# Layer 1's attention logits: rows added by TensorE, the bend split between ScalarE and VectorE

## The chip, the cores and the metric

The kernel runs on one core of one Trainium2 chip. The metric is the device time of one execution in microseconds, and the median of several executions is compared. The trace is of one execution of its own.

## The reference, cut to what matters

A network of four layers (a graph part and a feed-forward part in each) runs over 3125 nodes with 256 features and 50,000 edges sorted by destination. The change touches one part alone, the edges of layer 1's graph attention (4 heads of 64 features):

```
xl = x @ W_l + b_l          # per node, gathered by the edge's source
xr = x @ W_r + b_r          # per node, taken at the edge's destination
e  = xl[src] + xr[dst] + edge_attr_16 @ W_e
e  = leaky_relu(e, 0.2)     # "the bend"
logit = sum(e * att, over the 64 features of a head)
# then softmax of the logits over the edges of one destination,
# and the sum of xl[src] times those shares, per destination
```

## The kernel before, in words

The edges lie in slots, in pairs of 2 x 128 edges that belong to one block of 128 destinations. A batch is two pairs, that is 512 edges or four tiles of 128 (`BATCH` 4, `TWO` 2), and there are 110 batches. The function `gat_edges` does layer 1 (tiles named `l1e_`) and layer 3 (`l3e_`). It is written by hand as one instruction order for each engine. `skewed` takes a list of steps with lags and unrolls five batches in one loop round: in the round for batch t, a step of lag 2 works on batch t - 2. Semaphores tie the engines together, and each engine runs its own list strictly in order. A batch goes through these steps:

- SyncE loads the records (`l1e_rec`) and the edge attributes, turned and split in bf16 parts (`l1e_attrT`). GpSimd writes the indices of the sources, marks the first two tiles of the one-hot matrix of destinations (L1088), and issues four indirect DMAs that gather the rows of xl (`l1e_rows`, L1054). VectorE marks the other two tiles (L1096, "the one-hot half").
- TensorE turns the one-hot tiles (`l1e_ps_hot`). ScalarE copies them twice from PSUM (`l1e_outside` L3332 and `l1e_nodehot` L3333, "the one-hots' copies").
- TensorE sums xr[dst] (L3449) and the attribute part (L3450) into `l1e_ps_x`, 256 columns for each of four tiles ("the sums").
- VectorE adds the gathered rows (`join`, L3459), one instruction of 512 columns for each pair, and bends in place (`bend`, L3464), again one for each pair.
- GpSimd multiplies by the attention vector (L3481), and VectorE reduces to logits (L3486).
- TensorE turns the logits into rows, four units for each batch ("the logits' rows", L3291 and L3294, two head pairs for each of two pairs of tiles). VectorE takes the largest of each unit (L3208, "the tops"), raises the running top (L3216, L3223) and forms the factors by which old sums shrink (L3225, L3228, "the shrinks").
- TensorE spreads the tops back to the edges (L3311, "the spread"). VectorE subtracts them from the logits (L3233, L3236, "the fall"). ScalarE exponentiates (L3341) and weighs the gathered rows with 16 copies of 64 columns and 4 small ones (L3350, L3352, "the weighing").
- TensorE sums the weighted rows by destination (L3305, "the weighted sums"), VectorE adds them to the running totals (L3249), and ScalarE flushes these (L3366, L3367).

VectorE's order within one round is: one-hot half, tops of the first two units, raise, join of pair 0, tops of the last two units, raise and shrinks, join of pair 1, both bends, totals, fall, totals, logits. TensorE's is: rows of the logits of pair 1, weighted sums, spread, sums, rows of the logits of pair 0, turned one-hots. In any round the joins belong to the batch after the one whose tops are taken, and the sums on TensorE to the batch after that.

Of the kernel before, what the change touches and what calls it, by code (L numbers as in the profile page):

```python
# [12 lines left out]
ALU = mybir.AluOpType  # L13
ACT = mybir.ActivationFunctionType
# [998 lines left out]
class Gather:  # L1013
# [5 lines left out]
    def __init__(self, s, net, placed, table, width, lo):  # L1019
# [8 lines left out]
        self.half_ready = s.sem("half_ready")  # L1028
# [44 lines left out]
    def find(self, eng, q, i, b):  # L1073

        eng.wait_ge(self.rec_loaded[b], i * 16 + 16)
        eng.tensor_copy(self.idx[b][:, :], self.column(b, self.placed.far)).then_inc(self.idx_ready, 1)  # L1076
# [4 lines left out]

    def hot_tiles(self, eng, q, i, b, tick):
        eng.wait_ge(self.rec_loaded[b], i * 16 + 16)
        eng.wait_ge(self.hot_free, q + 1)
        eng.sem_inc(tick, 1)
        eng.tensor_copy(self.idx[b][:, :], self.column(b, self.placed.far)).then_inc(self.idx_ready, 1)
        for k in range(BATCH // 2):
            ins = eng.tensor_scalar(at(self.onehot[b], k, P), self.net.columns[:, :], self.column(b, self.placed.near, k),  # L1088
                                    None, ALU.is_equal)
        ins.then_inc(self.hot_ready, 1)  # L1090

    def hot_half(self, eng, q, i, b):
        wide = [P, BATCH // 2, P]
        eng.wait_ge(self.rec_loaded[b], i * 16 + 16)
        eng.wait_ge(self.hot_free, q + 1)
        eng.tensor_tensor(tiled(self.onehot[b][:, :], P)[:, BATCH // 2:BATCH, :],  # L1096
                          self.net.columns[:, :].unsqueeze(1).to_broadcast(wide),
                          self.column(b, self.placed.near)[:, BATCH // 2:BATCH].unsqueeze(2).to_broadcast(wide), ALU.is_equal)\
            .then_inc(self.half_ready, 1)
# [2015 lines left out]
def gat_edges(net, name, heads, each, table, lo, logits_of, tops=None):  # L3115
# [11 lines left out]
    with ExitStack() as ctx:  # L3127
# [136 lines left out]
        def _(pe):  # L3264
# [5 lines left out]
            def turn(q, i, b):  # L3270
                pe.wait_ge(g.hot_ready, q + 1)
                if UNITS > 1:
                    pe.wait_ge(g.half_ready, q + 1)
# [48 lines left out]
        def _(act):  # L3322
# [46 lines left out]
            skewed(act, (3, shrinks), (3, weigh), (0, turn), (4, flush))  # L3369


class L1Logits:
# [5 lines left out]
    by_pair = True  # L3378

    def __init__(self, net, xr, att, s, g, ps_x, nodehot, logit, logit_ready, nodehot_ready):  # L3380
# [6 lines left out]
        self.e = [s.sb(f"e{k}", [P, 2 * D]) for k in range(TWO)]  # L3387
        self.loaded = s.sem("we_loaded")
# [19 lines left out]
    def gather(self, pool):  # L3408
        skewed(pool, (0, lambda q, i, b: self.g.hot_tiles(pool, q, i, b, self.pool_tick)), (0, lambda q, i, b: self.g.gather_batch(pool, q, b)),
               (2, lambda q, i, b: self.multiply(pool, q)))  # L3410
# [4 lines left out]
    def hot(self, dve, q, i, b):  # L3415
        self.g.hot_half(dve, q, i, b)
# [22 lines left out]
    def tensor(self, pe, q, i, b):  # L3439
# [837 lines left out]
```

## Time and profile before

| what | us |
|---|---|
| median of 3 runs | 6451.83 (6433.74 to 6451.86) |
| the profiled execution | 6440.41 |
| its span | 6439.0 |
| edges of layer 1: first sums to last logits | 2326.8 to 3401.8 |

| engine, whole span | busy |
|---|---|
| TensorE matmul | 76% |
| VectorE | 67% |
| TensorE weight load | 58% |
| GpSimd | 48% |
| ScalarE | 43% |

Shares over the whole span mix eight stages. The change lies in the stage of layer 1's edges alone, about a sixth of the time, so what counts is read there: how long a batch takes, which engine waits for which, and what is late last. The records of TensorE's matmuls last longer than the spacing of two of them, since they overlap in the pipe. The price of one more matmul is therefore taken from the spacing of starts and not from the mean record.

### The profile page before, as it was taken

The page shows a single profiled execution, that of the slowest core. Times are in us where ns is not written, and L with a number is a line of the kernel's source. Part 1 is how long each engine was busy: PE and PEld are TensorE (multiplying, and loading weights), DVE is VectorE, ACT ScalarE, POOL GpSimd, SP SyncE. Part 2 cuts the span into 40 slices and gives each one's busy share as a digit, 9 for nine tenths or more (in the row PEclk, how much of TensorE's full clock was granted, in tenths as well). Part 3 has the DMA queues.
Part 4 walks back from the last instruction along what each step waited for, and adds up shares of the span by engine and source line. Part 5 has one row for each costly group of instructions (what it writes and reads, how often), then busy time and mean ns, then how long its engine had stood idle before and what let it go on. Part 6 is the DMA issues. An engine that isn't in the chain of part 4 may idle for free. (4 is left out here: it accounts for less than half of the span.)

```text
span 6439.0 us, 120316 instructions
## 1 busy us (share of the span) xinstructions
PE 4915.4 (76%) x25586; PEld 3702.7 (58%) x25587; DVE 4325.7 (67%) x13269; ACT 2736.8 (43%) x8015; POOL 3093.6 (48%) x3493
## 2 busy tenths in 40 slices
PE   5621999994574578888883899969989997888595
PEld 4510777763453356666663566645657775666484
DVE  7770888873786679999997777753433335888613
ACT  0010877773114336666662111124523333887421
POOL 4786777776474048888880222213210001777221
PEclk9975999997696689999995899989989998999697
DMA  6522444455586222222231555543520002666453
GB/s 237 179 65 58 122 120 121 120 113 102 137 252 150 62 57 70 66 70 68 68 66 48 167 186 187 183 129 113 147 79 10 10 10 66 161 159 159 75 172 108
DMA packets 843340, 719.85 MB, mean 112 GB/s; under 512 B 405662, under 2 KB 749251, under 8 KB 842660
## 3 DMA queue, kind: packets, MB, share of 16 engines
q1 hardware_dynamic: 596280, 372.06, 20.5%
q0 software_dynamic: 120064, 280.26, 16.7%
q10 hardware_dynamic: 126828, 65.67, 3.5%
q8 instruction: 59, 0.97, 0.1%
q14 instruction: 109, 0.89, 0.0%
HBM read 521.19 MB, written 201.60 MB: 112 GB/s over the span
## 5 line engine op out<-in xcount | busy, mean ns | idle before, releaser
L1054 POOL DMA_INDIRECT l3e_rows<-table,l3e_idx x440 | 436.0, 991 | 736.6 <-DVE l3e_idx L1076 608.9
L1054 POOL DMA_INDIRECT l0e_rows<-table,l0e_idx x440 | 448.8, 1020 | 150.0 <-issue 132.0
L1054 POOL DMA_INDIRECT l1e_rows<-table,l1e_idx x440 | 430.6, 979 | 121.4 <-issue 121.4
L3350 ACT ACTIVATE l1e_weighted<-l1e_rows,l1e_power 128x64 f32<-128x64 f32 x1760 | 462.9, 334 | 16.7 <-ACT l1e_power L3341 9.3
L824 POOL DMA_INDIRECT records_by_src<-l0n_rec_src,l0n_pos_at_src x390 | 399.4, 1024 | 115.3 <-issue 109.1
L1331 PE MATMUL l0e_ps_w<-l0e_wf,l0e_hidT 128*128 128x256 f32 x1760 | 417.3, 391 | 34.8 <-DVE l0e_shifted L1272 34.7
L1331 PEld LDWEIGHTS l0e_ps_w<-l0e_wf,l0e_hidT 128*128 128x128 f32 x1760 | 331.3, 193 | 162.5 <-issue 87.0
L3291 PE MATMUL l1e_ps_row<-net_ident,l1e_logit 128*128 128x128 f32 x1760 | 276.8, 280 | 128.9 <-DVE l1e_logit L3486 127.5
L2673 ACT ACTIVATE l1fg_hT<-l1fg_ps_h,l1fg_b_cols 128x256 f32<-128x256 f32 x256 | 107.5, 471 | 530.0 <-PE l1fg_ps_h L2616 529.9
L2055 ACT ACTIVATE l2fe_hT<-l2fe_ps_h,l2fe_own,l2fe_own 128x320 f32<-128x320 f32 x320 | 197.6, 618 | 309.7 <-PE l2fe_ps_h L2005 309.4
L3305 PE MATMUL l3e_ps_s<-l3e_weighted,l3e_onehot 128*128 128x257 f32 x880 | 250.4, 430 | 92.2 <-ACT l3e_weighted L3352 92.2
L3481 POOL TENSOR_TENSOR l1e_e<-l1e_e,l1x_att 128x512 f32<-128x512 f32 x220 | 274.8, 1271 | 84.9 <-DVE l1e_e L3464 84.8
L3291 PEld LDWEIGHTS l1e_ps_row<-net_ident,l1e_logit 128*128 128x128 f32 x1760 | 192.5, 137 | 209.7 <-issue 154.7
L2108 DVE SCALAR_TENSOR_TENSOR net_x<-l2fe_ps_y,l2fe_mix,net_x 128x256 f32 x200 | 96.8, 484 | 309.0 <-PE l2fe_ps_y L2017 309.0
L3851 PE MATMUL l2d_ps<-l2d_wide,net_work 128*128 128x512 f32 (+2 forms) x800 | 290.1, 518 | 8.3 <-DVE l2d_wide L3902 5.9
L2788 POOL DMA_INDIRECT outputs<-l1fg_y,l1fg_target x64 | 70.5, 1102 | 467.5 <-DVE l1fg_y L2725 455.9
L3208 DVE TENSOR_REDUCE l1e_tile_top<-l1e_ps_row 128x2 f32<-128x512 f32 x440 | 287.3, 685 | 4.2 <-PE l1e_ps_row L3294 2.7
L2616 PE MATMUL l1fg_ps_h<-l1fg_xT,l1fg_w_in 128*128 128x256 f32 x1024 | 264.8, 381 | 1.7 <-DVE l1fg_xT L2713 0.8
L3449 PE MATMUL l1e_ps_x<-l1x_xr,l1e_nodehot 128*128 x880 | 255.7, 393 | 2.7 <-ACT l1e_nodehot L3333 2.7
L3305 PEld LDWEIGHTS l3e_ps_s<-l3e_weighted,l3e_onehot 128*128 128x128 f32 x880 | 162.9, 204 | 159.4 <-ACT l3e_weighted L3352 141.9
L3769 POOL DMA_DIRECT2D l2d_counts<-counts x192 | 108.2, 564 | 279.2 <-ACT l2d_wide L3961 139.8
L2630 PE MATMUL l1fg_ps_y<-l1fg_w_out,l1fg_hT 128*128 128x256 f32 x1024 | 231.2, 379 | 0.0
(830 smaller groups left out, 14840.9 us busy)
## 6 DMA issues: line engine op xcount, KB each, us to landing
counts<-l1f_total ACTq DMA_DIRECT2D x272, 128.0 KB, 4.0
l1fg_w_in<-in_L_ffn_W SPq DMA_DIRECT2D x32, 1024.0 KB
l1fg_w_out<-in_L_ffn_W SPq DMA_DIRECT2D x32, 1024.0 KB
records_by_dst<-l0n_blank_dst SPq DMA_DIRECT2D x5, 6512.0 KB
l3e_rec<-records_by_dst SPq DMA_DIRECT2D x110, 296.0 KB, 3.1
l2d_counts<-counts SPq DMA_DIRECT2D x208, 128.0 KB, 2.7
l2d_counts<-counts POOLq DMA_DIRECT2D x192, 128.0 KB, 2.8
l3fg_w_in<-in_L_ffn_w SPq DMA_DIRECT2D x16, 1024.0 KB, 7.5
```

The source lines that it names most:

```text
L824: pool.indirect_dma_start(self.to.records, bass.IndirectOffsetOnAxis(self.pos_at[b][:, j:j + 1], 0), at(self.rec[b], j, self.to.width), No ...
L1054: pool.indirect_dma_start(at(self.rows[b], k, self.width), None, self.table, bass.IndirectOffsetOnAxis(self.idx[b][:, k:k + 1], 0)).then_i ...
L1331: ins = pe.matmul(ps_w[:, k, m * D:(m + 1) * D], hidT[b][:, c * WIDE + (2 * k + m) * P:c * WIDE + (2 * k + m + 1) * P], at(wf2, c, D), sta ...
L2616: ins = pe.matmul(ps_h[:, n % HALVES, (m % 2) * SLICE:(m % 2 + 1) * SLICE], w_in[b][:, c * F + m * P:c * F + (m + 1) * P], at(xT[b], c, SL ...
L2630: ins = pe.matmul(ps_y[:, t, 0:D], hT[b][:, c * SLICE + t * P:c * SLICE + (t + 1) * P], at(w_out[b], c, D), start=c == 0, stop=c == FC - 1)
L3208: dve.tensor_reduce(tile_top[:, c:c + w], tiled(ps_row[:, side, 0:w * PAIR], PAIR), AX.X, ALU.max)\
L3291: pe.matmul(ps_row[:, side, lo:lo + P], logit[b][:, c:c + 1].to_broadcast([P, P]), net.ident[:, :], is_transpose=True, start=h == h0 and m ...
L3305: ins = pe.matmul(ps_s[:, k, 0:W], at(g.onehot[b], m, P), at(weighted, m, W), start=m == 2 * k, stop=m > 2 * k)
L3350: act.activation(out[:, h, 0:each], g.rows[b][:, lo:lo + each], ACT.Copy, scale=power[b][:, m * heads + h:m * heads + h + 1])
L3449: pe.matmul(out, at(self.nodehot[b], 2 * k + m, P), at(self.xr, self.block[k], D), start=True, stop=False)
L3481: pool.tensor_tensor(e, e, self.att[:, :].unsqueeze(1).to_broadcast([P, 2, D]), ALU.mult).then_inc(self.times_att, 1)
L3851: ins = pe.matmul(ps[0:k_in, n % 2, 0:width(g)], lhsT, wide[k % WIDE][:, 0:width(g)], start=t == 0, stop=False)
```

## The change

Four things change, all in layer 1's edges:

1. TensorE adds the gathered rows. After the two products for a tile comes a third, the identity times the tile's rows (f32, 256 columns), into the same PSUM sum. There are four more products for each batch, and TensorE waits for the gathered rows first.
2. ScalarE takes the positive part: for each pair one Relu with scale 0.8 from `l1e_ps_x` into a new tile `l1e_above`. This step stands between the weighing and the one-hots' copies.
3. VectorE has one join for each pair: 0.2 times the PSUM sum plus `l1e_above`. Adding the rows and the two bends are gone. GpSimd's multiply waits for this join.
4. The one-hot is marked whole by VectorE (128x512 in one instruction, L1009) and no longer half by GpSimd.

```diff
 class Gather:
-    def hot_tiles(self, eng, q, i, b, tick):      # indices, two tiles of the one-hot
-    def hot_half(self, eng, q, i, b):             # the other two
+    def find(self, eng, q, i, b, tick=None):      # indices alone
 ...
             def turn(q, i, b):                    # TensorE
                 pe.wait_ge(g.hot_ready, q + 1)
-                if UNITS > 1:
-                    pe.wait_ge(g.half_ready, q + 1)
 ...
-            skewed(act, (3, shrinks), (3, weigh), (0, turn), (4, flush))
+            skewed(act, (3, shrinks), (3, weigh), *([(1, lambda q, i, b: logits.bend(act, q, i, b))] if logits.bends else []),
+                   (0, turn), (4, flush))
 ...
 class L1Logits:
     def gather(self, pool):
-        skewed(pool, (0, lambda q, i, b: self.g.hot_tiles(pool, q, i, b, self.pool_tick)), (0, lambda q, i, b: self.g.gather_batch(pool, q, b)),
+        skewed(pool, (0, lambda q, i, b: self.g.find(pool, q, i, b, self.pool_tick)), (0, lambda q, i, b: self.g.gather_batch(pool, q, b)),
                (2, lambda q, i, b: self.multiply(pool, q)))
     def hot(self, dve, q, i, b):
-        self.g.hot_half(dve, q, i, b)
+        dve.wait_ge(self.g.rec_loaded[b], i * 16 + 16)
+        self.g.hot(dve, q, i, b)
     def tensor(self, pe, q, i, b):
+        self.g.wait_rows(pe, i, b)
         for k in range(TWO):
             n = q * TWO + k
             pe.wait_ge(self.x_read, n + 1)
             for m in range(2):
                 out = self.ps_x[:, k, m * D:(m + 1) * D]
                 pe.matmul(out, at(self.nodehot[b], 2 * k + m, P), at(self.xr, self.block[k], D), start=True, stop=False)
-                ins = pe.matmul(out, at(self.attrT[b], 2 * k + m, P), self.we_parts[:, :], start=False, stop=True)
+                pe.matmul(out, at(self.attrT[b], 2 * k + m, P), self.we_parts[:, :], start=False, stop=False)
+                ins = pe.matmul(out, self.net.ident[:, :], at(self.g.rows[b], 2 * k + m, D), start=False, stop=True)
             ins.then_inc(self.sums, 1)
-    def join(self, dve, q, b, k):
-        dve.wait_ge(self.sums, q * TWO + k + 1)
-        dve.tensor_tensor(self.e[k][:, :], self.ps_x[:, k, 0:2 * D], at(self.g.rows[b], k, 2 * D), ALU.add).then_inc(self.x_read, 1)
-    def bend(self, dve, q, k):
-        e = self.e[k][:, :]
-        dve.wait_ge(self.x_read, q * TWO + TWO + k + 1)
-        dve.scalar_tensor_tensor(e, e, self.SLOPE, e, ALU.mult, ALU.max).then_inc(self.bent, 1)
+    def bend(self, act, q, i, b):
+        for k in range(TWO):
+            act.wait_ge(self.sums, q * TWO + k + 1)
+            act.activation(self.above[k][:, :], self.ps_x[:, k, 0:2 * D], ACT.Relu, scale=1.0 - self.SLOPE).then_inc(self.bent, 1)
+    def join(self, dve, q, k):
+        dve.wait_ge(self.bent, q * TWO + k + 1)
+        dve.scalar_tensor_tensor(self.e[k][:, :], self.ps_x[:, k, 0:2 * D], self.SLOPE, self.above[k][:, :], ALU.mult, ALU.add)\
+            .then_inc(self.x_read, 1)
     def multiply(self, pool, q):
-        pool.wait_ge(self.bent, q * TWO + TWO)
+        pool.wait_ge(self.x_read, q * TWO + 2 * TWO)
```

TensorE, the sums of one pair of tiles, of the kernel before and then of the changed one:

```order
L3449 MATMUL l1e_ps_x<-l1x_xr,l1e_nodehot 128x256
L3450 MATMUL l1e_ps_x<-l1e_we_parts,l1e_attrT 128x256
L3449 MATMUL l1e_ps_x<-l1x_xr,l1e_nodehot 128x256
L3450 MATMUL l1e_ps_x<-l1e_we_parts,l1e_attrT 128x256
L3446 REGISTER_ALU
```

```order
L3434 MATMUL l1e_ps_x<-l1x_xr,l1e_nodehot 128x256
L3435 MATMUL l1e_ps_x<-l1e_we_parts,l1e_attrT 128x256
L3436 MATMUL l1e_ps_x<-l1e_rows,net_ident 128x256
L3434 MATMUL l1e_ps_x<-l1x_xr,l1e_nodehot 128x256
L3435 MATMUL l1e_ps_x<-l1e_we_parts,l1e_attrT 128x256
L3436 MATMUL l1e_ps_x<-l1e_rows,net_ident 128x256
L3431 REGISTER_ALU
```

One product with the identity has come in for each tile, two for each pair and four for each batch. Nothing else of TensorE's order has moved.

ScalarE, the end of the weighing and what follows it, before and then changed (`l1e_above` is the positive part):

```order
L3350 ACTIVATE l1e_weighted<-l1e_rows,l1e_power 128x64 x4
L3352 ACTIVATE l1e_weighted<-l1e_power 128x4
L3331 ISA
L3332 ACTIVATE l1e_outside<-l1e_ps_hot 128x512
L3333 ACTIVATE l1e_nodehot<-l1e_ps_hot 128x512
```

```order
L3330 ACTIVATE l1e_weighted<-l1e_rows,l1e_power 128x64 x4
L3332 ACTIVATE l1e_weighted<-l1e_power 128x4
L3445 ISA
L3446 ACTIVATE l1e_above<-l1e_ps_x 128x512
L3445 REGISTER_ALU
L3446 ACTIVATE l1e_above<-l1e_ps_x 128x512
L3311 ISA
L3312 ACTIVATE l1e_outside<-l1e_ps_hot 128x512
L3313 ACTIVATE l1e_nodehot<-l1e_ps_hot 128x512
```

The two positive parts stand ahead of the copies, and the copies and the flush move back by two instructions.

VectorE, from the shrinks to the first tops of the next round, before and then changed:

```order
L3228 SCALAR_TENSOR_TENSOR l1e_shrink<-l1e_top,l1e_fresh 128x4
L3458 REGISTER_ALU
L3459 TENSOR_TENSOR l1e_e<-l1e_ps_x,l1e_rows 128x512
L3463 REGISTER_ALU
L3464 SCALAR_TENSOR_TENSOR l1e_e<-l1e_e 128x512
L3463 REGISTER_ALU
L3464 SCALAR_TENSOR_TENSOR l1e_e<-l1e_e 128x512
L3249 SCALAR_TENSOR_TENSOR l1e_total<-l1e_total,l1e_shrink,l1e_ps_s 128x65 x4
L3233 TENSOR_TENSOR l1e_ps_top<-l1e_logit,l1e_ps_top 128x16
```

```order
L3210 SCALAR_TENSOR_TENSOR l1e_shrink<-l1e_top,l1e_fresh 128x4
L3450 REGISTER_ALU
L3451 SCALAR_TENSOR_TENSOR l1e_e<-l1e_ps_x,l1e_above 128x512
L3231 SCALAR_TENSOR_TENSOR l1e_total<-l1e_total,l1e_shrink,l1e_ps_s 128x65 x4
L3215 TENSOR_TENSOR l1e_ps_top<-l1e_logit,l1e_ps_top 128x16
```

The two bends are gone from between the second join and the totals. The joins stand where they stood.

## Rows read from the trace of the kernel before

**Rows 1.** Busy time by stretch: PE, PEld, DVE, ACT, POOL (instructions), granted clock, DMA, GB/s.
```profile
2800.00:3000.00 200.00, 173.32 (x1072) 134.46 (x1072) 187.57 (x513) 139.30 (x583) 163.97 (x187) 1.00 0.27 68
```
**Rows 2.** Waits, 2400 to 3370 us: who for whom, total us, times, longest.
```profile
ACT l1e_power L3341 <- DVE l1e_power L3236: 214.6, 100, 2.7
...
PE l1e_ps_row L3291 <- DVE l1e_logit L3486: 107.6, 100, 1.4
...
PE l1e_ps_top L3311 <- DVE l1e_shrink L3228: 20.8, 100, 0.3
```
**Rows 3.** Timeline of VectorE, one batch: start, length, instruction.
```profile
2801.35 0.42 DVE L1096 TENSOR_TENSOR l1e_onehot<-net_columns,l1e_rec 128x256 f32<-128x256 f32 x1
2801.82 1.35 DVE L3208 TENSOR_REDUCE l1e_tile_top<-l1e_ps_row 128x2 f32<-128x512 f32 x2
...
2803.45 0.69 DVE L3459 TENSOR_TENSOR l1e_e<-l1e_ps_x,l1e_rows 128x512 f32<-128x512 f32 x1
2804.06 1.28 DVE L3208 TENSOR_REDUCE l1e_tile_top<-l1e_ps_row 128x2 f32<-128x512 f32 x2
...
2805.75 0.22 DVE L3228 SCALAR_TENSOR_TENSOR l1e_shrink<-l1e_top,l1e_fresh 128x4 f32<-128x4 f32 x1
2805.88 0.68 DVE L3459 TENSOR_TENSOR l1e_e<-l1e_ps_x,l1e_rows 128x512 f32<-128x512 f32 x1
2806.49 1.28 DVE L3464 SCALAR_TENSOR_TENSOR l1e_e<-l1e_e 128x512 f32<-128x512 f32 x2
2807.69 0.85 DVE L3249 SCALAR_TENSOR_TENSOR l1e_total<-l1e_total,l1e_shrink,l1e_ps_s 128x65 f32<-128x65 f32 x4
...
2808.66 0.17 DVE L3236 TENSOR_SCALAR l1e_power<-l1e_ps_top 128x16 f32<-128x16 f32 x1
...
2809.63 0.68 DVE L3486 TENSOR_REDUCE l1e_logit<-l1e_e 128x8 f32<-128x512 f32 x1
```
**Rows 4.** Timeline of TensorE (matmuls), the same batch.
```profile
2800.77 0.65 PE L3291 MATMUL l1e_ps_row<-net_ident,l1e_logit 128*128 128x128 f32 x4 [1.17 <-DVE l1e_logit L3486]
2801.25 0.38 PE L3294 MATMUL l1e_ps_row<-l1e_outside,l1e_ident_bf 128*128 128x512 bf16 x1
...
2803.92 1.92 PE L3305 MATMUL l1e_ps_s<-l1e_weighted,l1e_onehot 128*128 128x260 f32 x8
2806.02 1.05 PE L3311 MATMUL l1e_ps_top<-l1e_top,l1e_nodehot 128*128 128x4 f32 x8 [0.19 <-DVE l1e_shrink L3228]
2806.94 0.68 PE L3449 MATMUL l1e_ps_x<-l1x_xr,l1e_nodehot 128*128 x2
2807.45 0.27 PE L3450 MATMUL l1e_ps_x<-l1e_we_parts,l1e_attrT 128*128 128x256 bf16 x1
2807.56 0.60 PE L3449 MATMUL l1e_ps_x<-l1x_xr,l1e_nodehot 128*128 x2
...
2808.65 0.60 PE L3449 MATMUL l1e_ps_x<-l1x_xr,l1e_nodehot 128*128 x2
...
2810.45 0.65 PE L3291 MATMUL l1e_ps_row<-net_ident,l1e_logit 128*128 128x128 f32 x4 [1.10 <-DVE l1e_logit L3486]
```
**Rows 5.** Timeline of ScalarE: the exponential, and what follows the weighing.
```profile
2808.87 0.22 ACT L3341 ACTIVATE l1e_power<-l1e_power 128x16 f32<-128x16 f32 x1 [2.10 <-DVE l1e_power L3236]
...
2813.70 0.60 ACT L3332 ACTIVATE l1e_outside<-l1e_ps_hot 128x512 bf16<-128x512 f32 x1 [0.20 <-ACT l1e_weighted L3352]
2814.20 0.59 ACT L3333 ACTIVATE l1e_nodehot<-l1e_ps_hot 128x512 f32<-128x512 f32 x1
```
**Rows 6.** Groups by shape, whole span: count, busy us, mean ns, idle before.
```profile
L1009 DVE TENSOR_TENSOR l0e_onehot<-net_columns,l0e_rec 128x512 f32<-128x512 f32 x110 | 75.4, 685 | 0.0
L1263 DVE SCALAR_TENSOR_TENSOR l0e_hidT<-l0e_ps_h,l0e_bf_low,l0e_raised 128x512 f32<-128x512 f32 x220 | 154.4, 743 | 15.8 <-ACT l0e_raised L1371 14.5
L3333 ACT ACTIVATE l1e_nodehot<-l1e_ps_hot 128x512 f32<-128x512 f32 x110 | 65.1, 591 | 0.0
L1365 ACT ACTIVATE l0e_raised<-l0e_ps_h,l0e_bf 128x512 f32<-128x512 f32 x220 | 139.4, 684 | 34.3 <-PE l0e_ps_h L1322 33.7
```

More of the change, by code:

```diff
@@ L1027, in __init__ @@
         self.hot_ready = s.sem("hot_ready")
-        self.half_ready = s.sem("half_ready")
         self.rows_loaded = [s.sem(f"rows_loaded{b}") for b in range(RING)]
@@ L1071, in columns @@
         return self.rec[b][:, k * self.n + c:k * self.n + c + w]
-    def find(self, eng, q, i, b):
+    def find(self, eng, q, i, b, tick=None):
         eng.wait_ge(self.rec_loaded[b], i * 16 + 16)
+        if tick is not None:
+            eng.sem_inc(tick, 1)
         eng.tensor_copy(self.idx[b][:, :], self.column(b, self.placed.far)).then_inc(self.idx_ready, 1)
@@ L1080, in hot @@
         mark_nodes(eng, self.net, self.onehot[b], self.column(b, self.placed.near)).then_inc(self.hot_ready, 1)
-    def hot_tiles(self, eng, q, i, b, tick):
[L1083 to L1090, printed above, removed]
-    def hot_half(self, eng, q, i, b):
[L1093 to L1099, printed above, removed]
     def wait_rows(self, eng, i, b):
@@ L3378 @@
     by_pair = True
+    bends = True
     def __init__(self, net, xr, att, s, g, ps_x, nodehot, logit, logit_ready, nodehot_ready):
@@ L3387, in __init__ @@
         self.e = [s.sb(f"e{k}", [P, 2 * D]) for k in range(TWO)]
+        self.above = [s.sb(f"above{k}", [P, 2 * D]) for k in range(TWO)]
         self.loaded = s.sem("we_loaded")
@@ L3454, in vector_steps @@
         return self.vector_early, self.vector_middle, self.vector_late, self.find, self.hot
-    def join(self, dve, q, b, k):
-        dve.wait_ge(self.sums, q * TWO + k + 1)
-        dve.tensor_tensor(self.e[k][:, :], self.ps_x[:, k, 0:2 * D], at(self.g.rows[b], k, 2 * D), ALU.add).then_inc(self.x_read, 1)
-    def bend(self, dve, q, k):
-        e = self.e[k][:, :]
-        dve.wait_ge(self.x_read, q * TWO + TWO + k + 1)
-        dve.scalar_tensor_tensor(e, e, self.SLOPE, e, ALU.mult, ALU.max).then_inc(self.bent, 1)
+    def bend(self, act, q, i, b):
[6 more added lines that the diff above has]
+            .then_inc(self.x_read, 1)
     def vector_early(self, dve, q, i, b):
-        self.g.wait_rows(dve, i, b)
-        self.join(dve, q, b, 0)
+        self.join(dve, q, 0)
     def vector_middle(self, dve, q, i, b):
-        self.join(dve, q, b, 1)
+        self.join(dve, q, 1)
         dve.sem_inc(self.g.rec_free, 1)
-        self.bend(dve, q, 0)
-        self.bend(dve, q, 1)
     def multiply(self, pool, q):
-        pool.wait_ge(self.bent, q * TWO + TWO)
+        pool.wait_ge(self.x_read, q * TWO + 2 * TWO)
         pool.sem_inc(self.pool_tick, 1)
@@ L4040 @@
     by_pair = False
+    bends = False
     def __init__(self, net, wide, s, g, ps_x, nodehot, logit, logit_ready, nodehot_ready):
```

## The prediction

> **What bounds the kernel now.** I read the table of stretches first. In the stage that the change touches the clock is granted in full (1.00, the 2.4 GHz level), VectorE is busy 187.6 of 200 us, TensorE's matmuls 173.3, GpSimd 164.0 and ScalarE 139.3 [rows 1]. So VectorE looks like the bound, and a change that takes work from it looks right. But 94% busy is not a cycle, so I read the waits next: TensorE waits for the logits 107.6 us in 100 batches, and for the shrinks 20.8 us [rows 2]. Two engines hand the work to and fro, and what counts is the closed chain between them.
>
> The timeline gives that chain. I count from the first row of the logits on TensorE, 2800.77, as 0. The same row comes again at 2810.45 [rows 4], so a batch takes 9.68 us, and 110 batches take 1065 us (the count stands in [rows 6]). Within the batch:
> - 0.86: the first unit's rows are complete (2801.25 + 0.38) [rows 4].
> - 1.05: VectorE's first top starts, as the one-hot half before it ended at 1.00 (2801.77) [rows 3].
> - 1.05 to 5.25: tops, raise, join, tops, raise, shrinks in VectorE's order, until TensorE's spread starts at 2806.02 with a recorded wait of 0.19 for the shrink [rows 3, 4]. That is 4.20 us with no wait of VectorE.
> - 5.25 to 6.17: the spread, until the sums start at 2806.94 [rows 4].
> - 6.17 to 8.42: the sums. The last pair of products starts at 2808.65 and occupies 0.54, so TensorE is free at 2809.19 [rows 4].
> - 8.42 to 9.68: TensorE has nothing, 1.26 us. VectorE is still at the bends (1.28 recorded, 1.20 from start to start), totals, fall and logits [rows 3].
>
> So two things close together: VectorE's own list of 9.7 us, nearly without gaps, and TensorE's list, with 1.26 us of room at its end and 0.2 to 0.3 at the shrinks.
>
> **The change part by part.** All times are for one batch.
>
> *VectorE.* The two bends go: 1.20 (2806.49 to 2807.69) [rows 3]. The join becomes another operation of the same size, one operand in PSUM and one in SBUF. The join now costs 0.61 from start to start and 0.69 recorded [rows 3]. The nearest row of the new kind, in layer 0, costs 743 ns against 685 for a plain one, but it has a scalar in a tile where this one has a number [rows 6]. I take 0.61, with 0.67 as the upper bound. The one-hot grows from 0.42 to the 685 ns of the whole one [rows 3, 6], +0.27. VectorE's list falls from 9.68 to about 8.75, and VectorE no longer sets the pace.
>
> *ScalarE.* Two Relus of 128x512 from PSUM come in. The copy of the same shape takes 591 ns [rows 6] and the exponential with a bias tile 684 [rows 6]. I take 0.60 each, 1.2 in all. ScalarE was busy 139.3 of 200 us, 6.74 for a batch of 9.68 [rows 1], so there is room in total. What they can delay is checked below as a chain. The copies move back 1.2 us: in the walk below they end near 4.0, and the sums that read the turned one-hots begin at 6.0 and want those of a batch that was copied one round earlier. So that costs nothing. The flush behind them then ends near 5.6, before the next exponential at 6.7, which is covered by the 2.1 us that ScalarE waits for the fall now [rows 2, 5].
> The Trainium skill, "ScalarE: Activation LUTs", Rules for kernel authors, sends relu to VectorE and not to ScalarE, with a gain that it states for bf16. The f32 rows here don't bear that out: two bends on VectorE are recorded at 1.28 together [rows 3], and a copy from PSUM on ScalarE at 0.591 [rows 6]. By that page's budget for an ACTIVATE a Relu would be estimated at 0.72 us, which would lengthen the ScalarE chain by 0.12 and still not make it the longest.
>
> *GpSimd.* Its two tiles of the one-hot go, and its multiplies wait for the joins, which come earlier than the bends did. It loses work and gains nothing, so it costs nothing. The gathers keep their place: they are issued a round ahead of the sums that now read the rows, and their issue moves forward. So TensorE's new wait for the rows costs nothing in the steady state. If the rows were late, everything on TensorE would queue behind it (sums, logits' rows, turned one-hots).
>
> *TensorE.* Four f32 products of 256 columns come in. A pair of products (f32 and bf16) takes (2808.65 - 2807.56) / 2 = 0.545, and the bf16 one takes 0.11 of it (2807.45 to 2807.56) [rows 4]. So the f32 one is 0.435, and four are 1.74 us. Lower bound: were they as cheap as the bf16 ones, 4 x 0.11 = 0.44. Upper bound: the first product in the stretch takes 0.51 (2806.94 to 2807.45), so 2.04. I take 1.74, since the weights are f32 as in the row it comes from. No further weight load shows, as loads of the same size already hide behind such products.
>
> **The sum.** The closed chain, with the new prices:
> - first unit's rows complete at 0.86, first top starts at 0.91, since the one-hot is done long before. This saves 0.14 against 1.05.
> - 4.20 to the spread: 5.11.
> - 0.92 for the spread: 6.03.
> - 2.25 + 1.74 = 3.99 for the sums: 10.02.
> - The next logits' rows start at once if the logits are there. The second join starts at 4.97. Then 0.61, totals 0.77, fall 0.40, totals 0.77, first logits 0.68: 8.20. So the logits are 1.8 us early, and the one-hot behind them is done near 9.8, before the next first top at 10.93.
>
> The batch takes 10.02 against 9.68: +0.34, and times 110 it is +37 us. TensorE's wait for the logits vanishes (1.26), but 1.74 comes into the same place, and the saving of 0.14 at the first top covers only part of the difference. VectorE's 0.93 of relief buys nothing more, because VectorE then waits for TensorE.
>
> The ScalarE chain is the other candidate. From the end of the fall (2808.83) to the end of the weighing, where the copies start now (2813.70), it is 4.87 [rows 3, 5]. The first Relu and its hand-over are 0.64. From the join of pair 0 to the end of the fall it is 5.38 now (2803.45 to 2808.83) [rows 3], less 1.20 for the bends, 4.18. The sum is 9.69. This is shorter than 10.02, so the Relu is ready 0.33 before the join wants it.
>
> The start and end of the stage may add or take 2 us. The sum is made against the profiled execution, 6440.4 us, and gives 6477. That execution lies 11 us under the median of the three runs and within their spread. From the median the sum is 6489. I forecast 6482.
>
> **The rivals.**
>
> *A. No change: the wait at the shrinks goes too.* TensorE's own list without any wait is 3.15 from the logits' rows to the weighted sums (2800.77 to 2803.92), 1.77 for these (four products of 260 columns), 0.92 and 3.99: 9.83, less about 0.1 for a wait on a top inside it. With the ScalarE chain at 9.69 the batch would be 9.7 to 9.8, within 10 us of now: 6445 to 6455. For it: only 0.3 us separates the cases, and an f32 product at 0.35 instead of 0.435 would be enough. Against it: VectorE's 4.20 is a string of dependent steps with the join in the middle, and nothing in the change shortens it.
>
> *B. Faster: the busiest engine sets the pace.* VectorE at 94% falls to about 8.75 us a batch. If the added products hide in TensorE's gaps, the batch goes toward that: -0.93 x 110 = -102 us, 6338. It decides the outcome where the chain through TensorE drops under 9.5, which takes products at the lower bound of 0.11 each (chain 8.7), and a weighing that starts earlier as well. The rows speak against it: the same f32 product keeps 0.435 in three pairs in a row, and the ScalarE chain alone holds 9.69.
> The Trainium skill, "Perfetto Trace Analysis", Identifying the Most-Contended Engine, says to optimize the engine of highest occupancy first, and to judge TensorE not by its matmul busy time. By that rule VectorE is the engine to relieve. The waits of this trace [rows 2] put TensorE in the same closed chain.
>
> *C. Slower still: the Relus are late at the join.* A Relu of 0.684 like the exponential [rows 6], joins of 0.67 and a weighing slowed 5% (0.22) by sharing with the neighbours give 9.69 + 0.09 + 0.12 + 0.22 = 10.1, and a wait on it before the join shifts the tops and the spread behind it. With both chains hitting each other, 10.3 is plausible: +0.62 x 110 = +68, 6510 to 6520. For it: the slack is only 0.33 us. Against it: each bound would have to hold at once.
>
> **How the numbers follow.** A measurement of this kernel tells about 0.3%, 19 us, from no change. The forecast case, with 6465 to 6500 as its own range, has a chance of 0.61. Rival C has 0.15, A 0.16 and B 0.08. Slower by over 0.3% is all of C and most of the forecast case, 0.73. Within is A and the low edge of the forecast case, 0.18. Faster is 0.09. The range reaches over A's place and C's: 6444 to 6520. It leaves out B and the ends.
>
> **What would show it.** In the trace of the changed kernel: a batch of 10.0 us; the identity products spaced 0.43; TensorE's wait for the logits gone, its wait for the shrinks still there at 0.2 to 0.4 a batch; VectorE idle 1.2 to 1.5 us a batch before the tops, waiting for TensorE's logit rows, and busy near 81%; no wait of the joins for ScalarE. If the joins wait for the Relu, C is right. If TensorE shows no wait at all and the batch is 9.8, A is right. A batch under 9.5 would overturn the sum.

## The result and the profile after

| | before | after |
|---|---|---|
| median, us | 6447.03 (4 runs, 6433.74 to 6451.86) | 6484.43 (4 runs, 6480.44 to 6492.23) |
| profiled execution, us | 6440.41 | 6480.44 |
| TensorE, VectorE, ScalarE, GpSimd busy | 76, 67, 43, 48% | 79, 65, 44, 45% |
| one batch of layer 1's edges, median | 9.68 | 10.09 |

The ratio is 1.0068, 95% interval 1.0057 to 1.008: slower, by 0.7%. The forecast was 6482, +37 by the sum against the profiled execution; measured are +40.0 there and +37.4 in the medians.

In the traces the stage, from the end of the means' product ahead of it (the last write of `l1n_ps`) to the end of its last weighted sums, goes from 1115.3 us to 1154.2, +38.9. It falls into three parts. From the first spread to the last, 109 batches, it is 1057.1 before and 1098.8 after, +41.7. Behind the last spread nothing changes (8.2). Ahead of the first spread it is 50.0 before and 47.2 after, -2.8: the first sums come 3.8 us later, and the filling of the pipeline from there to the first logits takes 10.8 us instead of 16.6. Outside the stage about 1 us is left, but as the balance of two larger differences: the stages ahead of it are 7.4 us shorter in the second trace, and those behind it 8.3 us longer, though the change touches neither.

The table of stretches of the changed kernel, the same 200 us as [rows 1] and with the same columns:

```profile
2800.00:3000.00 200.00, 196.54 (x1191) 159.22 (x1189) 163.60 (x459) 152.51 (x592) 133.69 (x140) 1.00 0.26 66
```

VectorE fell from 187.6 to 163.6 us, and GpSimd from 164.0 to 133.7. TensorE rose from 173.3 to 196.5, 98% of the stretch. The clock is the same, so the busy times can be compared.

The waits of the changed kernel, from 2400 to 3400 us (who for whom, total, times, longest), to be read against [rows 2]:

```profile
POOL l1e_e L3466 <- DVE l1e_e L3451: 155.3, 99, 1.7
ACT l1e_power L3321 <- DVE l1e_power L3218: 144.2, 99, 1.5
DVE l1e_tile_top L3190 <- PE l1e_ps_row L3274: 132.0, 99, 1.4
...
POOL l1e_rows L1053 <- POOL l1e_idx L1077: 80.4, 99, 0.8
...
PE l1e_ps_top L3291 <- DVE l1e_shrink L3210: 17.2, 99, 0.2
```

The hand-over has turned round. Before, TensorE waited for VectorE's logits, 107.6 us in 100 batches. That wait is gone, and VectorE now waits for TensorE's logits' rows, 1.33 us a batch. The only wait of TensorE's matmuls is the one for the shrinks, 0.17 a batch. GpSimd has a new wait of 0.81 a batch between writing the indices and the first gather, since its one-hot tiles no longer stand between them. Nothing waits for the gathers, so it costs nothing.

VectorE's timeline of one batch, to be read against [rows 3]:

```profile
2800.56 1.34 DVE L3190 TENSOR_REDUCE l1e_tile_top<-l1e_ps_row 128x2 f32<-128x512 f32 x2 [1.24 <-PE l1e_ps_row L3274]
...
2802.19 0.69 DVE L3451 SCALAR_TENSOR_TENSOR l1e_e<-l1e_ps_x,l1e_above 128x512 f32<-128x512 f32 x1
2802.79 1.28 DVE L3190 TENSOR_REDUCE l1e_tile_top<-l1e_ps_row 128x2 f32<-128x512 f32 x2
...
2804.63 0.68 DVE L3451 SCALAR_TENSOR_TENSOR l1e_e<-l1e_ps_x,l1e_above 128x512 f32<-128x512 f32 x1
...
2806.20 0.17 DVE L3218 TENSOR_SCALAR l1e_power<-l1e_ps_top 128x16 f32<-128x16 f32 x1
...
2810.66 1.34 DVE L3190 TENSOR_REDUCE l1e_tile_top<-l1e_ps_row 128x2 f32<-128x512 f32 x2 [1.35 <-PE l1e_ps_row L3274]
```

TensorE's, the same batch, against [rows 4]:

```profile
2804.76 1.05 PE L3291 MATMUL l1e_ps_top<-l1e_top,l1e_nodehot 128*128 128x4 f32 x8 [0.18 <-DVE l1e_shrink L3210]
2805.68 0.68 PE L3434 MATMUL l1e_ps_x<-l1x_xr,l1e_nodehot 128*128 x2
2806.19 0.27 PE L3435 MATMUL l1e_ps_x<-l1e_we_parts,l1e_attrT 128*128 128x256 bf16 x1
2806.30 0.60 PE L3436 MATMUL l1e_ps_x<-l1e_rows,net_ident 128*128 128x256 f32 x2
2806.74 0.59 PE L3434 MATMUL l1e_ps_x<-l1x_xr,l1e_nodehot 128*128 x2
...
2809.66 0.60 PE L3271 MATMUL l1e_ps_row<-net_ident,l1e_logit 128*128 128x128 f32 x4
2810.10 0.38 PE L3274 MATMUL l1e_ps_row<-l1e_outside,l1e_ident_bf 128*128 128x512 bf16 x1
```

The chain reads: first top at 2800.56, spread at 2804.76 (4.20), sums at 2805.68 (0.92), logits' rows at 2809.66 (3.98) with no gap before them, next top at 2810.66 (1.00). That is 10.10. An identity product takes 2806.74 - 2806.30 = 0.44; over the four it is (3.98 - 2.25) / 4 = 0.43.

ScalarE's timeline, against [rows 5], and the groups by shape from 2400 to 3400 us, against [rows 6]:

```profile
2806.41 0.22 ACT L3321 ACTIVATE l1e_power<-l1e_power 128x16 f32<-128x16 f32 x1 [1.45 <-DVE l1e_power L3218]
...
2811.21 1.08 ACT L3446 ACTIVATE l1e_above<-l1e_ps_x 128x512 f32<-128x512 f32 x2 [0.19 <-ACT l1e_weighted L3332]
```

```profile
L3451 DVE SCALAR_TENSOR_TENSOR l1e_e<-l1e_ps_x,l1e_above 128x512 f32<-128x512 f32 x198 | 135.6, 685 | 0.0
...
L3446 ACT ACTIVATE l1e_above<-l1e_ps_x 128x512 f32<-128x512 f32 x198 | 107.4, 595 | 19.0 <-ACT l1e_weighted L3332 19.0
```

The Relu costs 595 ns, and the new join 685, as the old one did. Neither join waited for a Relu.

### The profile page after: what moved, and what is told of

It is laid out like the page before. It is cut to its first block and busy times, and to the rows that moved or that the text cites. A ratio compares the mean times of both kernels' runs of the same rounds, so it can differ in the third digit from the quotient of the medians.

```text
span 6478.8 us, 122003 instructions
## 1 busy us (share of the span) xinstructions
PE 5092.3 (79%) x26466; PEld 3875.8 (60%) x26467; DVE 4229.1 (65%) x13049; ACT 2848.6 (44%) x8235; POOL 2947.8 (45%) x3273
## 5 line engine op out<-in xcount | busy, mean ns | idle before, releaser
L1053 POOL DMA_INDIRECT l1e_rows<-table,l1e_idx x440 | 451.8, 1027 | 195.5 <-issue 105.7
L3330 ACT ACTIVATE l1e_weighted<-l1e_rows,l1e_power 128x64 f32<-128x64 f32 x1760 | 463.1, 334 | 10.7 <-ACT l1e_power L3321 3.7
L3434 PE MATMUL l1e_ps_x<-l1x_xr,l1e_nodehot 128*128 x880 | 271.9, 391 | 7.6 <-DMA l1e_rows<-table,l1e_idx 6.0
L3436 PE MATMUL l1e_ps_x<-l1e_rows,net_ident 128*128 128x256 f32 x880 | 263.4, 381 | 0.0
```

The costliest lines, as they stand in the source:

```text
L1053: pool.indirect_dma_start(at(self.rows[b], k, self.width), None, self.table, bass.IndirectOffsetOnAxis(self.idx[b][:, k:k + 1], 0)).then_i ...
L3330: act.activation(out[:, h, 0:each], g.rows[b][:, lo:lo + each], ACT.Copy, scale=power[b][:, m * heads + h:m * heads + h + 1])
L3436: ins = pe.matmul(out, self.net.ident[:, :], at(self.g.rows[b], 2 * k + m, D), start=False, stop=True)
```

## The experiments

My theory: the batch is the closed chain through TensorE, 10.10 us, of which the four identity products are 1.73. Behind it stands ScalarE's chain, 9.7. The rivals: the Relu on ScalarE, the join inside VectorE's 4.20, or the whole one-hot sets the time.

The kernels lay on different chips. On chip 12, and on the one of the first measurement, the kernel before takes 6446 and 6447 us. On chips 8, 9 and 11 it takes 7288, 7335 and 7311. Ratios are therefore always against the kernel before on the same chip, and the mechanism is read from the batch (start of one spread to the next), which for the kernel before is 9.68 on chip 8 too. The means are those of the 99 batches that remain without the first and the last five.

| kernel | chip | ratio (95%) | batch | mean |
|---|---|---|---|---|
| before, again | 8 | one run | most frequent 9.65, median 9.68 | 9.70 |
| changed, again | 12 | 1.0063 (1.0048, 1.0079) | median 10.09 | 10.09 |
| changed, again | 8 | 1.0158 (1.0119, 1.0196) | shortest 10.08, median 10.76 | 10.96 |
| no identity products | 11 | 1.0066 (1.0041, 1.009) | most frequent 9.66 | 10.23 |
| no identity products, again | 9 | 1.0038 (1.0016, 1.0061) | most frequent 9.66 | 10.24 |
| before + identity products | 11 | 1.0112 (1.0084, 1.014) | shortest 10.09, most frequent 10.48 | 10.56 |
| Relus behind the copies | 11 | 1.033 (1.0303, 1.0357) | shortest 11.02, most frequent 12.7 | 12.03 |
| joins behind the shrinks | 11 | 1.002 (1.0004, 1.0036) | most frequent 9.73 | 9.87 |
| the same in the kernel before | 8 | 1.0021 (1.0007, 1.0036) | most frequent 9.88 | 9.90 |
| one-hot halved again | 12 | 1.0062 (1.0047, 1.0077) | median 10.09 | 10.10 |
| half of the change | 8 | 0.9984 (0.9962, 1.0006) | median 9.52 | 9.55 |
| half of the change, joins in place | 12 | 0.9927 (0.9914, 0.9941) | most frequent 9.22 | 9.27 |

The changed kernel once more on chip 12 takes 6485.64 us beside 6445.53 of the kernel before, +40.1, where +35 to +45 was expected.

**Without the identity products.** The sum lacks the rows.

```diff
-                pe.matmul(out, at(self.attrT[b], 2 * k + m, P), self.we_parts[:, :], start=False, stop=False)
-                ins = pe.matmul(out, self.net.ident[:, :], at(self.g.rows[b], 2 * k + m, D), start=False, stop=True)
+                ins = pe.matmul(out, at(self.attrT[b], 2 * k + m, P), self.we_parts[:, :], start=False, stop=True)
```

> The changed kernel without the four identity products; the gathered rows are left out of the logits, all else stays. Theory (the closed chain through TensorE and the tops sets the changed kernel's batch of 10.10 us, and the identity products are 1.73 of it): that chain falls to 8.37, and the next chain sets the pace, the ScalarE one of 4.84 (fall to end of weighing) + 0.64 (Relu) + 4.18 (join to fall) = 9.66 us a batch, so 6484 - 48 = about 6436 us, ratio to before 0.998, with the joins now waiting for the Relu. Rival 1 (VectorE's own list of about 8.8 is next, the ScalarE chain was put too long): 6340 us. Rival 2 (the identity products cost little): 6475 or more.

The quiet batches take 9.66, as worked out for ScalarE's chain, and the joins wait for the Relus in about two thirds of all batches. The total missed: the ratio is 1.0066, where 0.998 was expected. In 34 of 99 batches the sums run slower, and 26 batches take about 11.5. The second run, on another chip, asks whether the clock is the cause.

> The kernel of e1_no_identity again (the changed kernel without the identity products; the gathered rows are left out of the logits), since e1 ran on a chip where TensorE's clock fell in a third of its batches, and the quiet batches were 9.66 us. Theory: where the granted clock stays 1.00, every batch is 9.66 us, set by the ScalarE chain, and the time is 6484 - 48 = 6436 us on a chip where the changed kernel takes 6484, ratio 0.998. Rival (the gap before the spread brings the clock down by itself, on any chip): batches of 11.5 us in between and a granted clock of 0.94 in the stage, ratio 1.005 or more.

The same again: slower sums in 32 of 99 batches, 29 of them at about 11.5, and a ratio of 1.0038. That is the rival's picture (its 0.94 and its 11.5 us), but this kernel has run on two chips only, both among the slower ones (the kernel before takes 7311 and 7335 us there). The table of stretches of this kernel, and of the kernel before run on chip 8:

```profile
3200.00:3400.00 200.00, 174.94 (x1017) 134.91 (x1018) 161.21 (x455) 151.66 (x593) 132.20 (x139) 0.94 0.25 65
```

```profile
3200.00:3400.00 200.00, 172.95 (x1073) 134.17 (x1071) 187.85 (x513) 141.52 (x585) 163.78 (x188) 1.00 0.26 67
```

Only the first lost clock (0.94). Its busy time is no smaller, 174.9 against 173.0, but part of that is instructions that last longer at the lower clock. TensorE's timeline of the first shows where:

```profile
3301.50 1.05 PE L3291 MATMUL l1e_ps_top<-l1e_top,l1e_nodehot 128*128 128x4 f32 x8 [1.36 <-issue]
3302.41 0.68 PE L3434 MATMUL l1e_ps_x<-l1x_xr,l1e_nodehot 128*128 x2
3302.93 0.37 PE L3435 MATMUL l1e_ps_x<-l1e_we_parts,l1e_attrT 128*128 128x256 bf16 x1
3303.09 1.06 PE L3434 MATMUL l1e_ps_x<-l1x_xr,l1e_nodehot 128*128 x2
3303.95 0.42 PE L3435 MATMUL l1e_ps_x<-l1e_we_parts,l1e_attrT 128*128 128x256 bf16 x1
3304.16 1.06 PE L3434 MATMUL l1e_ps_x<-l1x_xr,l1e_nodehot 128*128 x2
...
3306.29 0.65 PE L3271 MATMUL l1e_ps_row<-net_ident,l1e_logit 128*128 128x128 f32 x4
3306.78 0.38 PE L3274 MATMUL l1e_ps_row<-l1e_outside,l1e_ident_bf 128*128 128x512 bf16 x1
3307.00 0.60 PE L3271 MATMUL l1e_ps_row<-net_ident,l1e_logit 128*128 128x128 f32 x4
```

TensorE was idle 1.36 us, did the spread, and then a pair of products took 1.07 (3303.09 to 3304.16) instead of 0.54: the 1.2 GHz level. From 3306.29 on the spacing is that of the full clock again. The sums take 3.88 instead of 2.25. The long batches also hold a top of the last unit that starts about 1.4 late. In the kernel before the gap is about as long (1.0 to 1.4), but lies ahead of the logits' rows, and the clock holds. This suggests that the place of the gap decides, but the other batches of the same run speak against it as the whole reason:

```profile
3231.29 1.05 PE L3291 MATMUL l1e_ps_top<-l1e_top,l1e_nodehot 128*128 128x4 f32 x8 [1.62 <-DVE l1e_shrink L3210]
...
3240.88 1.06 PE L3291 MATMUL l1e_ps_top<-l1e_top,l1e_nodehot 128*128 128x4 f32 x8 [1.11 <-issue]
```

Here the gap ahead of the spread is 1.62, longer than in the slow batch, and the batch behind it takes 9.59 at full clock. Of the 99 batches 64 have such a gap of 1.05 to 1.79 and keep the clock, and 32 have one of 1.06 to 1.36 and lose it. Neither the place nor the length of that one gap tells them apart. The cause of the lost clock is open, and this kernel didn't run on chip 12.

**The kernel before with the identity products alone.** TensorE adds the rows and VectorE adds them a second time.

```diff
+        self.g.wait_rows(pe, i, b)
-                ins = pe.matmul(out, at(self.attrT[b], 2 * k + m, P), self.we_parts[:, :], start=False, stop=True)
+                pe.matmul(out, at(self.attrT[b], 2 * k + m, P), self.we_parts[:, :], start=False, stop=False)
+                ins = pe.matmul(out, self.net.ident[:, :], at(self.g.rows[b], 2 * k + m, D), start=False, stop=True)
```

> The kernel before with the four identity products and TensorE's wait for the rows added, nothing else; the joins add the rows as well, so that they are counted twice. Theory: the batch is set by 1.00 to the first top, 4.20 to the spread, 0.92, and 3.98 for the sums = 10.10 us, as in the changed kernel, because the relief of VectorE lies beside it: 6484 +- 8 us, ratio 1.006 to 1.008. VectorE would then have about 0.4 us of idle a batch and TensorE none for the logits. Rival (VectorE's relief also counts, since its list of 9.7 us and the longer sums add up in part): 10.3 us or more a batch, 6515 us or more.

The spreads at both ends of an undisturbed batch (10.11), and of a disturbed one (10.49):

```profile
3292.94 1.05 PE L3311 MATMUL l1e_ps_top<-l1e_top,l1e_nodehot 128*128 128x4 f32 x8 [0.28 <-issue]
...
3303.05 1.05 PE L3311 MATMUL l1e_ps_top<-l1e_top,l1e_nodehot 128*128 128x4 f32 x8 [0.19 <-DVE l1e_shrink L3225]
```

```profile
3523.35 1.05 PE L3311 MATMUL l1e_ps_top<-l1e_top,l1e_nodehot 128*128 128x4 f32 x8 [0.59 <-DVE l1e_shrink L3228]
...
3533.84 1.06 PE L3311 MATMUL l1e_ps_top<-l1e_top,l1e_nodehot 128*128 128x4 f32 x8 [0.57 <-DVE l1e_shrink L3228]
```

The total missed: the ratio is 1.0112, where 1.006 to 1.008 was expected, and the number is the rival's. The batches say why. In 45 of 99 the last top comes in time, and these take 10.09 to 10.26, the changed kernel's time or up to 0.17 more, with all of VectorE's work as before. In another 45 the last top starts 0.3 late (in the batch shown it is 0.93 behind the one before it, where 0.60 is usual), and they take 10.48 to 10.53. In 7 the sums run at half speed, 13.5 us. The pieces of the chain are the changed kernel's in both of the first groups (sums 3.98, first top 1.01 behind the rows, spread 0.91), and VectorE waits about 0.4 ahead of the tops, as worked out. So in undisturbed batches these products alone bring the new time, and taking 0.93 us a batch from VectorE moves it by 0.17 at most. The late last top is also in the changed kernel on chip 8 (below), so it isn't the price of VectorE's longer list alone. This kernel didn't run on chip 12, so that its total there isn't shown.

**The Relus behind the one-hots' copies.**

```diff
-            skewed(act, (3, shrinks), (3, weigh), *([(1, lambda q, i, b: logits.bend(act, q, i, b))] if logits.bends else []),
-                   (0, turn), (4, flush))
+            skewed(act, (3, shrinks), (3, weigh), (0, turn),
+                   *([(1, lambda q, i, b: logits.bend(act, q, i, b))] if logits.bends else []), (4, flush))
```

> The changed kernel with the two Relus behind the one-hots' copies instead of ahead of them. Theory (the ScalarE chain is 9.66 us with the Relu directly behind the weighing, 0.44 shorter than the batch): behind the copies it is 9.66 + 0.97 = 10.63 us and becomes the bound, +0.53 x 110 = +58, 6542 us, ratio 1.015, and the joins wait for the Relu. Rival (ScalarE has 1.45 us of waiting a batch, which takes up the delay): 6484 us, ratio 1.007.

ScalarE's and VectorE's timelines of this kernel, a stretch of one short batch:

```profile
3429.13 0.60 ACT L3312 ACTIVATE l1e_outside<-l1e_ps_hot 128x512 bf16<-128x512 f32 x1 [0.58 <-PE l1e_ps_hot L3256]
...
3430.10 1.09 ACT L3446 ACTIVATE l1e_above<-l1e_ps_x 128x512 f32<-128x512 f32 x2
```

```profile
3430.74 0.69 DVE L3451 SCALAR_TENSOR_TENSOR l1e_e<-l1e_ps_x,l1e_above 128x512 f32<-128x512 f32 x1 [0.83 <-issue]
```

Now the join stands 0.83 us and goes 0.64 after the Relu's start. The batch is 11.02 at least, not 10.63: the copies also wait 0.58 for the turned one-hots, which my sum had left out (0.39 of it is new, since 0.19 stood ahead of the Relu already). In 23 of 99 batches the last top is late as well (11.5), and in 52 the sums take 5.66 instead of 3.98, at half speed (12.7). The place of the Relus is what keeps ScalarE off the path: ahead of the copies they leave 0.4 us of room, behind them they cost 0.9 and more.

**The joins behind the shrinks.** In VectorE's order of the changed kernel the first join leaves the 4.20.

```diff
-                skewed(dve, hot, *units[:UNITS], (4, raise_first), early, *units[UNITS:], (4, raise_second), middle, *ends)
+                skewed(dve, hot, *units[:UNITS], (4, raise_first), *units[UNITS:], (4, raise_second), early, middle, *ends)
```

> The changed kernel with VectorE's first join moved from between the tops to behind the shrinks, so that it no longer lies between the logits' rows and the spread. Theory: that chain falls by 0.60 from 10.10 to 9.50, and TensorE's own list without waits, 3.12 + 1.77 + 0.92 + 3.98 = 9.79 less 0.1, becomes the bound: 9.7 to 9.8 us a batch, -36 to -44, 6440 to 6448 us, ratio 0.999 to 1.000. Rival (TensorE's list is already the bound, its recorded wait of 0.18 at the shrinks being no more than a hand-over): 6475 to 6484 us, ratio 1.006.

Most batches take 9.73 or 9.76, as forecast, and 9 of 99 take 10.6 to 10.7 with a late last top. VectorE and TensorE of this kernel:

```profile
3305.23 1.34 DVE L3190 TENSOR_REDUCE l1e_tile_top<-l1e_ps_row 128x2 f32<-128x512 f32 x2 [0.75 <-PE l1e_ps_row L3274]
3306.71 0.22 DVE L3198 SCALAR_TENSOR_TENSOR l1e_top<-l1e_top,l1e_fresh,l1e_tile_top 128x4 f32<-128x4 f32 x1
3307.02 1.35 DVE L3190 TENSOR_REDUCE l1e_tile_top<-l1e_ps_row 128x2 f32<-128x512 f32 x2
```

```profile
3307.33 1.92 PE L3285 MATMUL l1e_ps_s<-l1e_weighted,l1e_onehot 128*128 128x260 f32 x8
3309.08 1.02 PE L3291 MATMUL l1e_ps_top<-l1e_top,l1e_nodehot 128*128 128x4 f32 x8
3309.97 0.68 PE L3434 MATMUL l1e_ps_x<-l1x_xr,l1e_nodehot 128*128 x2
```

The spread now comes 3.85 after the first top instead of 4.20, and TensorE goes into it without a wait. This is rival A's state (TensorE's own list without any wait), reached only when the join leaves the string of dependent steps. The total is +0.2% (forecast -0.1% to 0), no gain over the kernel before. The kernel before with the same edit:

> The kernel before with the first join moved from between the tops to behind the shrinks, as in the experiment on the changed kernel, nothing else. Theory (before is bound by VectorE's list of 9.7 us, to which the order of its parts makes no difference): no change, within 8 us. Rival (the closed chain through TensorE bounds the kernel before as well): -0.6 us a batch, -66 us.

Missed: 9.88 instead of 9.68. Nor is it the rival's -0.6. In the kernel before, the join starts 0.15 after the raise and covers a hand-over. Without it in this place the second pair of tops starts 0.32 after the raise. The logits also wait 0.25 for GpSimd, where they waited 0.17.

**The one-hot halved again,** GpSimd marking two tiles as before, all else as changed.

> The changed kernel with one of its four parts undone: the one-hot's first two tiles on GpSimd and the others on VectorE, as before. Theory: neither engine sets the pace (VectorE waits for TensorE at the tops and gains 0.27 of waiting more, GpSimd 1.4 us less room), so the time of the changed kernel stays: within 8 us of c3_after_third in this job. Rival (GpSimd's gathers, which now come 1.4 us later, lay in VectorE's way): a shorter batch than the changed kernel by 0.2 us or more, -22 us.

10.09 and 1.0062, beside 10.09 and 1.0063 of the changed kernel on the same chip. The whole one-hot on VectorE costs nothing.

**The changed kernel on chip 8.**

> The changed kernel, unchanged, on the chip of these runs. Theory: batches of 10.10 us in the stage and a difference to before of +35 to +45 us wherever the whole time lies. Rival (the difference belongs to the first chip): a difference under 20 us or over 60.

Missed: the shortest batches take 10.08, but the mean is 10.96, and the difference to the kernel before is 124 us, over the rival's 60. So on chip 8 the change costs three times what it costs on chip 12. VectorE's timeline, then TensorE's, around one such place:

```profile
3306.78 0.68 DVE L3190 TENSOR_REDUCE l1e_tile_top<-l1e_ps_row 128x2 f32<-128x512 f32 x1
3308.03 0.69 DVE L3190 TENSOR_REDUCE l1e_tile_top<-l1e_ps_row 128x2 f32<-128x512 f32 x1 [0.57 <-PE l1e_ps_row L3274]
```

```profile
3306.45 0.38 PE L3274 MATMUL l1e_ps_row<-l1e_outside,l1e_ident_bf 128*128 128x512 bf16 x1
```

The last top starts 0.57 after its forerunner's end, although the rows it reads were complete at 3306.83. In 66 of 99 batches the last top is late by 0.6 to 0.8 like this (10.7 to 10.9 us), in 16 by 1.3 to 1.4 (11.4 to 11.5), and in 10 the sums run slower, most at 5.66 instead of 3.98 (11.8 us and more). Only 7 batches are undisturbed. I found no reason for the late tops in the trace. On chip 12 and in the first measurement they don't happen.

**Half of the change.** If four products are too many, two may fit into TensorE's 1.26 us of room: pair 1 takes the new way, pair 0 keeps the old one (add and bend on VectorE), the one-hot is halved as before.

```diff
+                ins = pe.matmul(out, at(self.attrT[b], 2 * k + m, P), self.we_parts[:, :], start=False, stop=k == 0)
+                if k:
+                    ins = pe.matmul(out, self.net.ident[:, :], at(self.g.rows[b], 2 * k + m, D), start=False, stop=True)
...
+        act.wait_ge(self.sums, q * TWO + 2)
+        act.activation(self.above[1][:, :], self.ps_x[:, 1, 0:2 * D], ACT.Relu, scale=1.0 - self.SLOPE).then_inc(self.bent, 1)
...
+        dve.tensor_tensor(self.e[0][:, :], self.ps_x[:, 0, 0:2 * D], at(self.g.rows[b], 0, 2 * D), ALU.add).then_inc(self.x_read, 1)
...
+        dve.scalar_tensor_tensor(e, e, self.SLOPE, e, ALU.mult, ALU.max).then_inc(self.bent0, 1)
```

> A version between the two: pair 0 of every batch as before (VectorE adds the rows and bends), pair 1 as changed (two identity products, one Relu, one join), the one-hot half on GpSimd as before, and the first join behind the shrinks. Theory: VectorE's list is 9.7 less one bend of 0.60 = 9.1, TensorE's without waits 9.79 - 0.87 = 8.9, GpSimd's 9.0, the ScalarE chain short since the join no longer precedes the tops: 9.1 to 9.2 us a batch against 9.68, -53 to -64 us against before, ratio 0.990 to 0.992. Rival (each added hand-over costs as much as the work saved): within 10 us of before.

With both joins behind the shrinks the median is 9.52, more than the 9.1 to 9.2 that I had worked out, and the ratio of 0.9984 is no clear gain (forecast 0.990 to 0.992). The kernel before had just shown what moving the first join uncovers, so it went back to its place (this run lay on another chip, so that the two differ in the chip as well):

> As e6_half (pair 0 of a batch as before, pair 1 as changed, the one-hot half on GpSimd), but with the first join left between the tops, since e5 and e6 showed that moving it uncovers hand-overs; the bend of pair 0 stands before the join of pair 1, and GpSimd waits for each pair apart. Theory: VectorE's list is 9.7 - 0.60 = 9.1 us, the closed chain through TensorE 1.00 + 4.20 + 0.92 + 3.12 = 9.24, and the larger sets the pace: 9.25 us a batch against 9.68, -47 us against before, ratio 0.993. Rival (uncovered hand-overs return as in e6_half): 9.45 us, -20 us, ratio 0.997.

9.22 (mean 9.27, forecast 9.25), and 6397.31 against 6445.53 us: 48 us less, where 47 were forecast. This beats both kernels. Its table of stretches, waits from 2400 to 3300 us, and TensorE's timeline:

```profile
2800.00:3000.00 200.00, 195.41 (x1207) 156.66 (x1206) 185.12 (x519) 153.44 (x621) 175.14 (x194) 1.00 0.28 72
```

```profile
PE l1e_ps_top L3313 <- DVE l1e_shrink L3230: 19.7, 97, 0.3
DVE l1e_logit L3500 <- POOL l1e_e L3495: 19.1, 81, 0.5
```

```profile
2803.13 1.05 PE L3313 MATMUL l1e_ps_top<-l1e_top,l1e_nodehot 128*128 128x4 f32 x8 [0.24 <-DVE l1e_shrink L3230]
2804.05 0.68 PE L3456 MATMUL l1e_ps_x<-l1x_xr,l1e_nodehot 128*128 x2
...
2807.17 0.60 PE L3293 MATMUL l1e_ps_row<-net_ident,l1e_logit 128*128 128x128 f32 x4
```

The sums take 3.12 = 2.25 + 0.87, the logits' rows start behind them without a gap, and TensorE (98%) and VectorE (93%) are both nearly full.

## Why the prediction was right, step by step

- First logits' rows to first top: forecast 0.91, measured 1.00 (2809.66 to 2810.66). This is the one term that was mis-sized. I had let the top start 0.05 after the end of the rows. Their end is 2810.10 + 0.38 = 2810.48, so the hand-over takes 0.18. The kernel before has it as well: its rows end at 2801.63 and its top starts at 2801.82, 0.19 later, and 94 of 100 batches lie between 0.18 and 0.22. I had put this time down to the one-hot half, and counted 0.14 of it as saved. Saved was 0.05, and 0.04 of that is in the rows themselves (0.82 instead of 0.86), which no longer start behind an idle TensorE.
- First top to spread: 4.20, measured 4.20. The spread: 0.92, measured 0.92.
- The sums: 3.99, measured 3.98, with the identity product at 0.43 (forecast 0.435). The lower bound of 0.11 and with it rival B are out.
- Together 10.02, measured 10.10. The totals are nearer to each other than the step allows, and part of that is luck. The batches between the first and the last spread add 41.7, not 37: the 0.08 makes 9 us more, and the means over all 109 of them, 9.70 and 10.08 instead of 9.68 and 10.10, take back 2 us each. The start of the stage gives back 2.8, and the untouched stages -7.4 and +8.3.
- The range 6444 to 6520 covers the places of A and C too, so that the total alone doesn't choose between the cases. The batch and the waits do.
- ScalarE's chain: 9.69. In the changed kernel it is 4.84 (end of the fall, 2806.37, to the first Relu, 2811.21), 0.64 and 4.18, 9.66. The 0.64, from a Relu to the join that waits for it, is measured in the kernel with the Relus behind the copies. The kernel without the identity products has batches of just this length, and there the joins of the quiet ones do wait for the Relu.
- VectorE's list: 8.75. Measured 10.10 - 1.35 of wait = 8.75.
- The waits: TensorE's for the logits gone, for the shrinks 0.17 recorded (0.2 to 0.4 forecast), VectorE's 1.33 (1.2 to 1.5), its share 82% (81%), no join waits for ScalarE.

Rival A needed TensorE without waits. The experiment with the joins moved shows it possible (9.73), but not in this order of VectorE's. Rival B fell with the price of the product. Rival C asked for late Relus. They weren't late, and the kernel with the Relus behind the copies shows what it would have cost: 11.02 and more, where I had put down 10.3. Of rival C's bounds none came: the Relu takes 0.595, the join 0.60 from start to start, and the weighing isn't slowed (4.84 against 4.87). The row of 684 ns from which I took the upper one isn't an exponential: L1365 is an absolute value with a bias tile.

## What to carry to other kernels

Relieving an engine that is 94% busy can still make a kernel slower: follow the hand-overs until the instruction comes round again, and price what the change adds to that closed chain. Moving work between engines pays up to the room on the receiving engine in its place in the chain (here 1.26 us: two products of 0.43 fit and give 0.7%, four don't and cost 0.7%). An order of instructions that covers a hand-over is part of the time, so when work moves, look at what had stood in front of it.

## What the runs showed of the hardware

- The kernel before takes 6446 us on chip 12, and 7288, 7335 and 7311 on chips 8, 9 and 11. Its batches in this stage are equally long on chip 8 (9.68). The difference lies in other stages, as far as the one trace from chip 8 shows: from 200 to 400 us of the span TensorE runs 374 instructions on chip 8, and 684 on the first chip. The cause is open.
- TensorE fell to the 1.2 GHz level behind an idle gap of 1.06 to 1.36 us ahead of the spread in 32 of 99 batches of the kernel without the identity products (busy 174.9 of 200 us, granted 0.94), while 64 batches of the same run kept the full clock behind gaps of 1.05 to 1.79. What tells them apart is open. The kernel before (173.0) keeps 1.00 with its gap ahead of the logits' rows. The changed kernel (196.5) and its half (195.4) keep it as well, the one in the first measurement and the other on chip 12. On chip 8 the changed kernel loses it in 10 of 99 batches, behind gaps of 1.48 to 1.57.
- The top of VectorE starts 0.18 us or more after the modelled end of TensorE's last row product, in every batch of the kernel before, the changed kernel and its half.
- An f32 product with the identity, 256 columns, occupies 0.43 to 0.44 us, and its bf16 neighbour of the same columns 0.11.
- A Relu of 128x512 f32 from PSUM takes 595 ns on ScalarE, as the copy does (591). VectorE takes 685 ns for the join, with its second operand in SBUF, and 683 ns for a bend. The Trainium skill, "ScalarE: Activation LUTs", Rules for kernel authors, sends relu to VectorE, with a gain that it states for bf16. These f32 rows show no such gain, but no run put the Relu itself on VectorE.
